# Attention and feed-forward block: value tiles 0 and 1 projected inside attention, output products of three groups ahead of the fourth division

## The chip, the cores and the metric

The kernel runs on one core of a Trainium2 chip, in one launch. The metric is the device time of that launch in microseconds (us). The median of three runs of the kernel before is the time to beat; a profiled execution gives the trace.

## What is computed

The block works on four sequences (B = 4) of 512 steps with 512 channels. In each of two stages a conditioning scan over time runs forward and backward in every channel and gives a ratio that is multiplied by a sigmoid of the input. The first stage is followed by causal attention with 16 heads of 32 channels, the second by a gated feed-forward layer with 2048 inner channels whose operands are quantised in blocks of 32. Cut to its core, the reference is:

```python
x = x + attn(cond(x, fside, fside, w, u, cond_512), w_qkv, w_o)
x = x + ffn(cond2(x, fside, fside, w2, u2, cond_512), w_gate, w_up, w_down)

# cond: nf, df are scans of ek*v and ek forward in time, nb, db backward
num = nf + nb - ekv + euk * vf
den = df + db - ek + euk
base = sigmoid(r) * (num / maximum(den, 1e-08))

# attn
q, k, v = split(einsum('bsh,oh->bso', hidden, w_qkv))
probs = softmax(where(causal, q @ k.T * scale, min))
out = einsum('bsh,oh->bso', probs @ v, w_o)

# ffn: every operand is rounded to a 4- or 6-bit grid with one power of two per block of 32
inter = silu(mx(x, w_gate)) * mx(x, w_up)
out = mx(inter, w_down)
```

## The kernel before

All arrays have the channels on the 128 partitions, in four chunks (`CJ = 4`), and time on the free axis. The program is written engine by engine with an order fixed by hand; semaphores join the engines. `turn(b, more)` exists on every engine and does sequence `b`, from the attention's second half of preparations to the output. `more` is false in the last turn (b = 3).

**Matmuls.** TensorE (PE) first does the scores by query of a head group (`scores`, six slots of a group, banks 0 to 3), whose maxima VectorE (DVE) takes (`maxima`). After `split_maxima` the maxima are transposed (`transpose_maxima`, bank 2), copied by ScalarE (ACT, `copy_maxima`), and used in the scores by key (`scores_by_key`, units n = 0 to 15 of a group, banks 4 and 5), which ACT turns into probabilities (`exps`). `weigh_values` multiplies the probabilities with the values `v_sb` and with ones into banks 6 and 7, and the division follows: a logarithm and an exponential on ACT (`sum_reciprocal`), three operations on DVE (`normalise`). Four groups (g = 0 to 3) run like this, and the six slots of the next group's `scores` stand between the units of the present one (`SLOT_BEHIND`). Groups 2 and 3 of the queries and keys are projected into banks 6 and 7 and copied out of there by `copy_raw`, which counts on `raw_copied`.

**The tail of a turn.** Behind the fourth group PE projects value tiles 0 and 1 of the next sequence, waits for the fourth division (`normed`), does the output projection (16 fp32 products of 128x512, each of which the trace shows as two instructions), value tiles 2 and 3, and queries and keys of group 0 of the next sequence. DVE adds each output chunk to `xt`, ACT takes its tanh (`tanh2`), DVE joins it to the second stage's ratio (`join`), makes the block scales and rounds. That sets `xq_ready`, for which the gate products (L1179) wait.

**The scans.** Between all of this DVE and ACT run the conditioning scans, unit by unit (`forward`, `backward`, `add_own`, `finish` on DVE, `weigh`, `reciprocals`, `own_exp` on ACT). Units 4 to 7 of a turn make `h` of the next sequence, units 8 to 11 the second stage's ratios of that sequence. In the last turn none of them is done. `h` is one buffer: SyncE (SP) loads `x[b + 1]` into it as soon as the queries and keys of turn b have been projected, and ACT takes its tanh behind group 0's exponentials.

GpSimd (POOL) makes two low parts at the head of a turn and issues half of the DMAs that place queries and keys in `stacks`.

## Time and profile before

| | |
|---|---|
| median of three runs | 1052.24 us (1050.89 to 1053.39) |
| profiled execution, time | 1056.65 us |
| profiled execution, span of the core | 1054.8 us |
| mean granted TensorE clock | 0.913 of full |
| PE busy | 729.8 us (69%) |
| DVE busy | 852.9 us (81%) |
| ACT busy | 414.6 us (39%) |
| shares of the chain that ended last | PE 42%, DVE 39%, issue 11%, ACT 7% |

The span runs from the first to the last instruction of the core. Busy times of engines overlap. The chain is followed back from the last instruction, at each step to what released it. A row of the timeline gives the start in us from the span's start, the length, the engine, the line of the kernel, the operation with output and inputs, how many instructions are merged (x), and in brackets the idle time of the engine ahead of it with what ended that. The granted clock is a share of 2.4 GHz; 0.50 is 1.2 GHz. The first 245 us of the span prepare the weights; the turns begin at about 245, 449, 656 and 861 us.

### The profile page before, as it was taken

The page shows a single profiled execution, that of the slowest core. Times are in us where ns is not written, and L with a number is a line of the kernel's source. Part 1 is how long each engine was busy: PE and PEld are TensorE (multiplying, and loading weights), DVE is VectorE, ACT ScalarE, POOL GpSimd, SP SyncE. Part 2 cuts the span into 40 slices and gives each one's busy share as a digit, 9 for nine tenths or more (in the row PEclk, how much of TensorE's full clock was granted, in tenths as well). Part 3 has the DMA queues.
Part 4 walks back from the last instruction along what each step waited for, and adds up shares of the span by engine and source line. Part 5 has one row for each costly group of instructions (what it writes and reads, how often), then busy time and mean ns, then how long its engine had stood idle before and what let it go on. Part 6 is the DMA issues. An engine that isn't in the chain of part 4 may idle for free.

```text
span 1054.8 us, 10177 instructions
## 1 busy us (share of the span) xinstructions
PE 729.8 (69%) x3680; PEld 366.4 (35%) x3680; DVE 852.9 (81%) x1160; ACT 414.6 (39%) x698; POOL 94.2 (9%) x151
## 2 busy tenths in 40 slices
PE   0000003835787899978789999778899996987566
PEld 0000001313454444445444444445344444553222
DVE  5999999997899678898984788979858988532577
ACT  3010110313676435247663361465643515452140
POOL 1000000001310000131100001311000032200000
PEclk9999999877699999988968999878899997999688
DMA  8411211034340000364300004732000065400001
GB/s 328 174 66 40 90 50 40 24 76 128 87 105 11 21 0 11 80 210 97 93 21 11 1 10 101 212 97 71 21 10 1 11 161 126 113 1 0 1 1 40
DMA packets 30306, 72.24 MB, mean 68 GB/s; under 512 B 5808, under 2 KB 5808, under 8 KB 28464
## 3 DMA queue, kind: packets, MB, share of 16 engines
q1 hardware_dynamic: 19792, 46.94, 14.9%
q0 software_dynamic: 6144, 16.79, 6.7%
q10 hardware_dynamic: 4320, 7.87, 2.3%
q8 instruction: 29, 0.48, 0.2%
q14 instruction: 21, 0.17, 0.1%
HBM read 33.82 MB, written 4.19 MB: 36 GB/s over the span
## 4 chain that ended last, share of the span: by engine, by line
PE 42%; DVE 39%; issue 11%; ACT 7%; DMA 1%; SPq 0%; ACTq 0%; DVEq 0%
PE bank L1179 11%; PE bank L1158 5%; PE bank L1119 5%; PE bank L1046 4%; PE bank L1103 4%; PE bank L1053 3%; PE bank L1079 3%; DVE region L691 3%; DVE negmax L866 2%; ACT region L475 2%; PE bank L1104 2%; DVE ratio L670 2%; DVE region L671 2%; DVE num L769 2%; DVE ratio L645 2%
## 5 line engine op out<-in xcount | busy, mean ns | idle before, releaser
L1046 PE MATMUL bank<-wqkv,h 128*128 128x512 f32 x128 | 60.0, 623 | 179.5 <-DVE h L803 171.0
L1103 PE MATMUL bank<-stacks 128*128 128x512 f32 (+3 forms) x256 | 115.8, 454 | 50.6 <-ACT region L475 42.0
L273 POOL DMA_DIRECT2D stacks<-rows x128 | 70.1, 555 | 778.4 <-DVE region L671 384.1
L866 DVE TENSOR_REDUCE negmax<-bank 128x4 f32<-128x512 f32 (+2 forms) x96 | 99.3, 1035 | 43.2 <-PE bank L1081 42.9
L475 ACT ACTIVATE region<-bank 128x512 f32<-128x512 f32 (+3 forms) x256 | 101.6, 433 | 81.1 <-PE bank L1105 80.3
L1053 PE MATMUL bank<-h,wqkv 128*128 128x512 f32 x256 | 113.7, 595 | 4.2 <-DVE region L1011 4.2
L1046 PEld LDWEIGHTS bank<-wqkv,h 128*128 128x128 f32 x128 | 25.2, 201 | 211.1 <-issue 201.7
L1079 PE MATMUL bank<-stacks 128*128 128x128 f32 (+3 forms) x256 | 94.6, 449 | 5.6 <-DVE negmax L866 4.4
L1104 PE MATMUL bank<-maxrow,pick 128*128 128x512 bf16 (+3 forms) x256 | 90.5, 353 | 0.0
L1103 PEld LDWEIGHTS bank<-stacks 128*128 128x128 f32 x256 | 56.5, 221 | 84.3 <-ACT region L475 62.1
L410 ACT ACTIVATE rec<-den 128x512 f32<-128x512 f32 x32 | 20.1, 630 | 145.6 <-DVE den L780 144.5
L1179 PE MATMUL bank<-region,gate_q 128*128 128x512 bf16 x256 | 62.2, 387 | 14.2 <-DVE region L671 14.2
L1191 PE MATMUL bank<-region,down_q 128*128 128x512 bf16 x256 | 59.0, 387 | 16.2 <-DVE region L671 16.2
L1053 PEld LDWEIGHTS bank<-h,wqkv 128*128 128x128 f32 x256 | 47.9, 190 | 60.6 <-issue 54.5
L1011 DVE TENSOR_TENSOR region<-bank,region 128x1024 f32<-128x1024 f32 x32 | 39.0, 1219 | 31.7 <-PE bank L1179 31.7
L1079 PEld LDWEIGHTS bank<-stacks 128*128 128x128 f32 x256 | 58.0, 229 | 14.4 <-issue 6.8
L1081 PE MATMUL bank<-hide_qk,identb 128*128 128x128 bf16 x256 | 62.4, 249 | 0.0
L1105 PE MATMUL bank<-hide_kq,identb 128*128 128x128 bf16 x256 | 62.0, 242 | 0.0
L1179 PE MATMUL bank<-region,up_q 128*128 128x512 bf16 x256 | 61.5, 384 | 0.0
L1158 PE MATMUL bank<-rows,wo 128*128 128x512 f32 x128 | 57.4, 607 | 3.5 <-DVE rows L884 3.5
L394 ACT ACTIVATE fd<-fd,omd_all 128x511 f32<-128x511 f32 x32 | 22.9, 716 | 93.5 <-DVE fd L752 93.5
L1119 PE MATMUL bank<-region,v_sb 128*32 128x128 f32 (+3 forms) x512 | 54.3, 485 | 1.8 <-ACT region L475 1.8
(126 smaller groups left out, 1378.8 us busy)
## 6 DMA issues: line engine op xcount, KB each, us to landing
stacks<-rows SPq DMA_DIRECT2D x128, 128.0 KB, 4.0
stacks<-rows POOLq DMA_DIRECT2D x128, 128.0 KB, 3.8
kt<-in_fside ACTq DMA_DIRECT2D x30, 256.0 KB, 3.1
h<-in_x SPq DMA_DIRECT2D x4, 1024.0 KB, 7.6
region<-in_w_gate SPq DMA_DIRECT2D x4, 1024.0 KB, 12.0
xt<-in_x SPq DMA_DIRECT2D x4, 1024.0 KB, 7.0
region<-in_w_up SPq DMA_DIRECT2D x4, 1024.0 KB, 5.6
region<-in_w_down SPq DMA_DIRECT2D x4, 1024.0 KB, 4.7
```

The lines of the kernel that those rows point to most:

```text
L273: eng.dma_start(stacks[HD * r:HD * r + HD, at:at + 2, i, :].bitcast(F32), rows[mine, q:k + 1:k - q, :]).then_inc(stacked[s][i], 16)
L475: nc.scalar.activation(probs[:, i, P_AT[t]:P_AT[t] + CAUSAL[t]], bank[4 + n % 2][:, 0:CAUSAL[t]], ACT.Exp, scale=SCALE).then_inc(p_ready, 1)
L866: nc.vector.tensor_reduce(o, scored, AX_X, ALU.max, negate=True).then_inc(max_taken, 1)
L1046: mm = nc.tensor.matmul(bank[4 + t % 2][:, :], h[:, j, P * t:P * t + P], wqkv[:, j, 2 * C:3 * C], start=(j == 0), stop=(j == CJ - 1))
L1053: mm = nc.tensor.matmul(qk_banks(g)[s][:, :], wqkv[:, j, C * s + P * g:C * s + P * g + P], h[:, j, :], start=(j == 0), stop=(j == CJ - 1))
L1079: nc.tensor.matmul(o[:, c:c + w], qs[s][:, i, P * t:P * t + P], ks[s][:, i, 0:w], start=True, stop=False, skip_group_check=True)
L1081: mm = nc.tensor.matmul(o[:, c + P * t:c + w], identb[:, :], hide_qk[:, :], start=False, stop=True, skip_group_check=True)
L1103: nc.tensor.matmul(o, ks[s][:, i, P * t:P * t + P], qs[s][:, i, P * t:T], start=True, stop=False)
L1104: nc.tensor.matmul(o, pick[:, i, :], maxrow[:, s, P * t:T], start=False, stop=False)
L1119: mm = nc.tensor.matmul(o[HD * i:HD * i + HD, P * t:T], w, probs[:, i, P_AT[t]:P_AT[t] + CAUSAL[t]], start=(t == 0), stop=(t == TT - 1), t ...
L1158: mm = nc.tensor.matmul(bank[j][:, :], wo[:, g, P * j:P * j + P], attn[g], start=(g == 0), stop=(g == GROUPS - 1))
L1179: mm = nc.tensor.matmul(bank[4 * (f % 2) + o + i][:, :], w[:, j, at:at + P], xq[:, j, :], start=(j == 0), stop=(j == CJ - 1))
```

## The change

- `project_values` now does one tile. Tiles 2 and 3 are projected where they were (and in the prologue), tiles 0 and 1 inside the attention part of the turn that uses them: tile 0 behind the last slot of group 0's `scores` and ahead of `transpose_maxima(b, 0)`, tile 1 behind unit 9 of group 0's `scores_by_key`. They go to banks 6 and 7 (`value_bank`) and wait for `raw_copied`.
- ACT copies tile 0 behind `copy_maxima(b, 0)` and tile 1 behind group 0's last exponentials. `weigh_values` of group 0 waits for both copies (`v_copied`) where it waited for `raw_copied`.
- The output projection is done by `project_out`: the products of groups 0 to 2 of chunks 0 and 1 come ahead of the first product that waits for the fourth division, and each chunk's fourth product comes behind the next chunk's first three.
- On DVE, unit 8's `backward` and `add_own` stand ahead of `normalise(b, 3)`.
- SP loads `h` of the next sequence when all four value tiles of the present one are done (`v_ready`), and it issues group 2's stack DMAs ahead of that wait.

```diff
+        def value_bank(t):
+
+            return bank[4 + t % 2] if t >= 2 else bank[6 + t]
...
+                stack(sp, b, 2, 0, 2)
                 if more:
-                    sp.wait_ge(qk_ready, b * (2 * GROUPS) + 2 * GROUPS)
+                    sp.wait_ge(v_ready, b * TT + TT)
                     sp.dma_start(h[:, :, :], x[b + 1]).then_inc(h_in, 16)
-                for g in range(2, GROUPS):
-                    stack(sp, b, g, 0, 2)
+                stack(sp, b, 3, 0, 2)
...
                 copy_maxima(b, 0)
+                copy_values(b, (0,))
                 weigh(b, 3, 1)
...
                 exps(b, 0, 10, 16)
+                copy_values(b, (1,))
                 weigh(b, 4, 0)
...
                 own_exp(b, 9)
-                if more:
-                    copy_values(b + 1, 0, 2)
...
                 cap(b, 9)
-                normalise(b, 3)
                 backward(b, 8, 0)
                 backward(b, 8, 1)
                 add_own(b, 8)
+                normalise(b, 3)
...
+            def project_values(b, t):
+
+                if t >= 2:
+                    pe.wait_ge(h_ready, b * CJ + CJ)
+                else:
+                    pe.wait_ge(raw_copied, 2 * b + 2)
...
-                        pe.wait_ge(raw_copied, 2 * b + 2)
+                        pe.wait_ge(v_copied, b * TT + TT)
...
+            def project_out(b, j, groups):
+
+                for g in groups:
+                    if g == GROUPS - 1:
+                        pe.wait_ge(normed, b * GROUPS + GROUPS)
+                    mm = nc.tensor.matmul(bank[j][:, :], wo[:, g, P * j:P * j + P], attn[g],
+                                          start=(g == 0), stop=(g == GROUPS - 1), skip_group_check=True)
+                if g == GROUPS - 1:
+                    mm.then_inc(proj_ready, 1)
...
                 scores(b, 0, 5)
+                project_values(b, 0)
                 transpose_maxima(b, 0)
...
+                        if g == 0 and n == 9:
+                            project_values(b, 1)
...
+                for j in range(CJ):
+                    project_out(b, j, range(GROUPS - 1))
+                    if j:
+                        project_out(b, j - 1, (GROUPS - 1,))
+                project_out(b, CJ - 1, (GROUPS - 1,))
                 if more:
-                    project_values(b + 1, 0, 2)
-                pe.wait_ge(normed, b * GROUPS + GROUPS)
-                for j in range(CJ):
-                    for g in range(GROUPS):
-                        mm = nc.tensor.matmul(bank[j][:, :], wo[:, g, P * j:P * j + P], attn[g],
-                                              start=(g == 0), stop=(g == GROUPS - 1))
-                    mm.then_inc(proj_ready, 1)
-                if more:
-                    project_values(b + 1, 2, TT)
+                    for t in (2, 3):
+                        project_values(b + 1, t)
```

On PE, at the tail of turn 0, behind the last products with the values, before the change (`wqkv,h` are value products, `rows,wo` output products):

```order
L1119 MATMUL bank<-region,ones 32x128 x4
L1046 MATMUL bank<-wqkv,h 128x512 [waits h_ready]
L1046 MATMUL bank<-wqkv,h 128x512 x7
L1158 MATMUL bank<-rows,wo 128x512 [waits normed]
L1158 MATMUL bank<-rows,wo 128x512 x15
L1046 MATMUL bank<-wqkv,h 128x512 [waits v_copied,h_ready]
L1046 MATMUL bank<-wqkv,h 128x512 x3
```

The same place on PE after the change:

```order
L1124 MATMUL bank<-region,ones 32x128 x4
L1135 MATMUL bank<-rows,wo 128x512 x6
L1135 MATMUL bank<-rows,wo 128x512 [waits normed]
L1135 MATMUL bank<-rows,wo 128x512 x3
L1135 MATMUL bank<-rows,wo 128x512 [waits normed]
L1135 MATMUL bank<-rows,wo 128x512 x3
L1135 MATMUL bank<-rows,wo 128x512 [waits normed] x2
L1051 MATMUL bank<-wqkv,h 128x512 [waits h_ready]
```

Eight value products are gone from here, and six output products now stand ahead of the first wait for the division.

On PE, at the head of turn 0, between group 0's last scores and its first unit by key, before the change:

```order
L1079 MATMUL bank<-stacks_49 128x512
L1081 MATMUL bank<-hide_qk,identb 128x128
L1088 MATMUL bank<-identb,negmax_hl 8x128 [waits max_split]
L1088 MATMUL bank<-identb,negmax_hl 8x128 x3
L1103 MATMUL bank<-stacks_49 128x512 [waits qk_low,mt_copied]
```

The same place on PE after the change:

```order
L1084 MATMUL bank<-stacks_49 128x512
L1086 MATMUL bank<-hide_qk,identb 128x128
L1051 MATMUL bank<-wqkv,h 128x512 [waits raw_copied]
L1051 MATMUL bank<-wqkv,h 128x512 x3
L1093 MATMUL bank<-identb,negmax_hl 8x128 [waits max_split]
L1093 MATMUL bank<-identb,negmax_hl 8x128 x3
L1108 MATMUL bank<-stacks_49 128x512 [waits qk_low,mt_copied]
```

Value tile 0 stands between the scores and the transposes, and it waits for ACT's raw copy.

On DVE, at the tail of turn 0, after the change (`rows<-bank,rsum` and its two neighbours are the division, `den`, `num` and `ekv` unit 8):

```order
L743 TENSOR_SCALAR ek<-kt 128x512 [waits fwd_ready,k_in1]
L773 SCALAR_TENSOR_TENSOR den<-decay_all,fd 128x512 [waits weighted,fwd_ready,h_ready,divided]
L773 SCALAR_TENSOR_TENSOR num<-decay_all,fn 128x512 [waits fwd_ready,weighted]
L782 SCALAR_TENSOR_TENSOR ekv<-eu,kt 128x512 [waits eu_ready]
L784 SCALAR_TENSOR_TENSOR den<-eu,den 128x512 [waits bwd_ready]
L787 TENSOR_TENSOR num<-num,ekv 128x512 [waits bwd_ready,euv_ready]
L884 TENSOR_TENSOR rows<-bank,rsum 128x512 [waits rsum_ready]
L886 SCALAR_TENSOR_TENSOR rsum<-rows,rsum 128x512 [waits refined]
L888 SCALAR_TENSOR_TENSOR rows<-bank,rsum 128x512 [waits refined]
L997 TENSOR_TENSOR xt<-bank,xt 128x512 [waits proj_ready,x_in]
```

The three rows of the division stood ahead of the five rows of unit 8 and now stand behind them.

## Rows read from the trace of the kernel before

**Rows 1.** Windows of attention, turn 1 and turn 3: length, busy time of each engine.

```profile
480.00:548.00 68.00, 55.54 (x428) 31.70 (x426) 64.06 (x86) 45.79 (x89) 8.46 (x16) 0.89 0.28 70
...
900.00:950.00 50.00, 45.98 (x412) 27.45 (x404) 22.31 (x31) 23.65 (x57) 5.62 (x11) 1.00 0.23 54
```

**Rows 2.** The chain that ended last, turn 1's tail: start, length, what.

```profile
554.94 7.05 PE bank L1119 x64
...
561.99 7.06 PE bank L1046 x16
...
569.05 13.73 PE bank L1158 x32
...
582.79 6.87 PE bank L1046 x16
...
596.52 1.81 PE bank L1059 x4
```

**Rows 3.** Timeline of PE, turn 3's tail: start, length, what, idle before it.

```profile
958.26 15.70 PE L1158 MATMUL bank<-rows,wo 128*128 128x512 f32 x32 [3.55 <-DVE rows L884]
...
988.17 3.59 PE L1179 MATMUL bank<-region,gate_q 128*128 128x512 bf16 x8 [14.21 <-DVE region L671]
```

**Rows 4.** Timeline of DVE, turn 1's tail.

```profile
563.34 0.69 DVE L880 TENSOR_TENSOR rows<-bank,rsum 128x512 f32<-128x512 f32 x1 [8.14 <-ACT rsum L492]
...
568.84 0.68 DVE L783 TENSOR_TENSOR num<-num,ekv 128x512 f32<-128x512 f32 x1
...
576.57 1.22 DVE L755 TENSOR_TENSOR_SCAN fn<-decay_all,ekv 128x512 f32<-128x512 f32 x1
...
581.03 0.69 DVE L985 SCALAR_TENSOR_TENSOR ratio<-region,ratio 128x512 f32<-128x512 f32 x1 [0.95 <-ACT region L575]
...
582.89 0.69 DVE L993 TENSOR_TENSOR xt<-bank,xt 128x512 f32<-128x512 f32 x1 [0.71 <-PE bank L1158]
...
595.73 1.23 DVE L671 TENSOR_TENSOR region<-ratio,region 128x2048 bf16<-128x2048 bf16 x1
```

**Rows 5.** Timeline of ACT, turn 1's tail.

```profile
571.89 1.06 ACT L437 ACTIVATE v_sb<-bank 128x512 f32<-128x512 f32 x2
```

**Rows 6.** Timeline of ACT, PE and DVE at turn 1's head.

```profile
465.50 1.00 ACT L463 ACTIVATE rows<-bank 128x1024 f32<-128x1024 f32 x1
...
469.14 0.80 PE L1103 MATMUL bank<-stacks 128*128 128x512 f32 x1 [2.13 <-ACT maxrow L469]
...
466.19 0.17 DVE L873 TENSOR_TENSOR negmax_hl<-negmax,negmax_hl 128x16 bf16<-128x16 f32 x1
...
480.47 0.68 DVE L780 SCALAR_TENSOR_TENSOR den<-eu,den 128x512 f32<-128x512 f32 x1
```

**Rows 7.** Timeline of DVE, turn 2's head.

```profile
673.10 0.17 DVE L873 TENSOR_TENSOR negmax_hl<-negmax,negmax_hl 128x16 bf16<-128x16 f32 x1
...
686.20 0.68 DVE L780 SCALAR_TENSOR_TENSOR den<-eu,den 128x512 f32<-128x512 f32 x1
```

**Rows 8.** Windows of one us: busy times, PEclk is the granted clock.

```profile
478.00:479.00 1.00, 1.00 (x10) 0.75 (x9) 0.09 (x1) 0.99 (x3) 0.00 (x0) 0.91 0.06 16
...
679.00:680.00 1.00, 1.00 (x9) 0.95 (x9) 1.00 (x1) 0.00 (x0) 0.97 (x1) 0.72 0.00 0
...
962.00:963.00 1.00, 1.00 (x2) 0.34 (x1) 0.00 (x0) 0.00 (x0) 0.00 (x0) 0.56 0.00 0
```

**Rows 9.** Timeline of PE: thirteenth unit of group 0, turns 1 to 3.

```profile
484.55 0.50 PE L1103 MATMUL bank<-stacks 128*128 128x512 f32 x1 [3.05 <-ACT region L475]
...
690.27 0.80 PE L1103 MATMUL bank<-stacks 128*128 128x512 f32 x1 [4.08 <-ACT region L475]
...
896.00 0.50 PE L1103 MATMUL bank<-stacks 128*128 128x512 f32 x1 [2.10 <-ACT region L475]
```

**Rows 10.** Instructions on h, 450 to 562 us: its load's time to landing.

```profile
DMA to landing us min/median/max: 8.3/8.3/8.3
```

**Rows 11.** Timeline of ACT: the tanh of h in turn 1.

```profile
491.65 1.92 ACT L518 ACTIVATE h<-h 128x2048 f32<-128x2048 f32 x1
```

More of the change, by code:

```diff
@@ L433, in _, with copy_values @@
             table(6)
-            def copy_values(b, first, last):
-                for t in range(first, last):
-                    act.wait_ge(v_ready, b * TT + t + 1)
-                    nc.scalar.activation(v_sb[:, t, :], bank[4 + t % 2][:, :], ACT.Copy).then_inc(v_copied, 1)
+            def copy_values(b, tiles):
+                for t in tiles:
+                    act.wait_ge(v_ready, b * TT + VALUE_ORDER.index(t) + 1)
+                    nc.scalar.activation(v_sb[:, t, :], value_bank(t)[:, :], ACT.Copy).then_inc(v_copied, 1)
             def high_parts(b, g):
@@ L576, in turn @@
                 if more:
-                    copy_values(b + 1, 2, TT)
+                    copy_values(b + 1, (2, 3))
                     high_parts(b + 1, 0)
@@ L618, in _ @@
                 if u == 8:
-                    copy_values(0, 0, TT)
+                    copy_values(0, (2, 3))
                     high_parts(0, 0)
@@ L1039, in _ @@
         def _(pe):
-            def project_values(b, first, last):
-                pe.wait_ge(h_ready, b * CJ + CJ)
-                for t in range(first, last):
-                    if t >= 2:
-                        pe.wait_ge(v_copied, b * TT + t - 1)
-                    for j in range(CJ):
-                        mm = nc.tensor.matmul(bank[4 + t % 2][:, :], h[:, j, P * t:P * t + P], wqkv[:, j, 2 * C:3 * C],
-                                              start=(j == 0), stop=(j == CJ - 1))
-                    mm.then_inc(v_ready, 1)
+            def project_values(b, t):
[4 more added lines that the diff above has]
+                for j in range(CJ):
+                    mm = nc.tensor.matmul(value_bank(t)[:, :], h[:, j, P * t:P * t + P], wqkv[:, j, 2 * C:3 * C],
+                                          start=(j == 0), stop=(j == CJ - 1))
+                mm.then_inc(v_ready, 1)
             def project_qk(b, g, s):
@@ L1151, in turn @@
                         scores(b, g + 2, 1)
-                if more:
-                    project_values(b + 1, 0, 2)
-                pe.wait_ge(normed, b * GROUPS + GROUPS)
-                for j in range(CJ):
-                    for g in range(GROUPS):
-                        mm = nc.tensor.matmul(bank[j][:, :], wo[:, g, P * j:P * j + P], attn[g],
-                                              start=(g == 0), stop=(g == GROUPS - 1))
-                    mm.then_inc(proj_ready, 1)
-                if more:
-                    project_values(b + 1, 2, TT)
+                for j in range(CJ):
+                    project_out(b, j, range(GROUPS - 1))
+                    if j:
+                        project_out(b, j - 1, (GROUPS - 1,))
+                project_out(b, CJ - 1, (GROUPS - 1,))
+                if more:
+                    for t in (2, 3):
+                        project_values(b + 1, t)
                     for s in range(2):
@@ L1198, in _ @@
             pe.wait_ge(weights_in, 32)
-            project_values(0, 0, TT)
+            for t in (2, 3):
+                project_values(0, t)
             for s in range(2):
@@ L1203, in _ @@
                 leave_low(0, 0, s)
-            pe.wait_ge(v_copied, TT)
+            pe.wait_ge(v_copied, 2)
             for s in range(2):
@@ L1216 @@
 HIGHS, LOWS = 6, 6
+VALUE_ORDER = (2, 3, 0, 1)
 SLOT_BEHIND = ({1: 0, 3: 1, 6: 2, 9: 3, 12: 4, 15: 5}, {3: 2, 7: 3, 11: 4, 15: 5})
```

2 lines of the change are left out of this document (1 added, 1 removed).

## The prediction

> **What bounds the kernel now.** I read first the chain that ended last, then the windows by stage, then the timelines at the two places where the order changes. The turns differ inside. Through most of attention in turns 0 to 2 DVE is the bound: busy 64.06 of 68 us in turn 1, PE 55.54. In turn 3, without scans of a next sequence, DVE has 22.31 us of work in 50, and PE with 45.98 is the bound [rows 1]. At a tail the chain lies on PE alone: values times probabilities until 561.99, two value tiles (7.06), the output projection (13.73), two more value tiles (6.87), then queries, keys and low parts until 598.33, where the gate products begin [rows 2]. Turns 0 and 2 have the same pieces to 0.1 us. In turn 3 nothing fills the wait: PE idles 3.55 us for the division, the projection takes 15.70 us in place of 13.73, and PE then idles 14.21 us for `xq_ready` [rows 3].
>
> **The tail, turns 0 to 2.** I count from T, the end of the last weighing of values (561.99). Removed from PE is 7.06 us. One product costs 13.73/16 = 0.86. Six products now fill 5.15 us. The division needs 3.5 us from T (the idle time of [rows 3]), so it comes in time. It also needs DVE to be free. Unit 8's two scans and three additions, which now stand ahead of it, take from 565.4 to 569.5, 4.1 us, and DVE has a hole of 8.14 us ahead of the division [rows 4], so they cost nothing. Were the hole gone, the division would be up to 4.1 us late, of which 5.15 - 3.5 = 1.65 is covered.
>
> The projection ends at T + 13.7. The chunks are ready after 7, 11, 15 and 16 products: T + 6.0, 9.4, 12.9 and 13.7. PE's remaining fill is 598.33 - 582.79 = 15.54 us [rows 2], so PE could begin the gates at T + 29.3. The other chain runs over DVE and ACT. Unit 9's second forward scan comes 0.6 us behind the addition of chunk 1, so at T + 10.2, and ends at T + 11.4. Behind it ACT weighs the scan, does `cap_exp`, loads a table and takes the first tanh. From the scan's end (576.57 + 1.22) to the first join (581.03) that took 3.2 us [rows 4]. The first join follows at T + 14.6 and takes until 15.8 (from 581.03 to 582.2), and only then comes the addition of chunk 3. From that addition to the end of the rounding it took 596.96 - 582.89 = 14.07 [rows 4]. So `xq_ready` comes at T + 29.9, 0.6 us behind PE. Before it was T + 36.3. Each of three tails gains 6.4 us: 19.2.
>
> **The tail, turn 3.** T is 954.7. The gates began at 988.17, T + 33.5 [rows 3]. There is no unit 9 and the table is loaded early, so the join of chunk 0 begins right after the addition of chunk 2, at T + 13.7, chunk 3 is added at T + 14.8 and the gates begin at T + 28.9. Gain 4.6, of which 3.5 is the filled wait and 2.0 the low clock behind it, less 0.9 because chunks 2 and 3 now come 0.86 us apart. Sum of the tails: 19.2 + 4.6 = 23.8.
>
> **The head: value tile 0.** It doesn't fill the idle time in which it stands. PE is done with the scores about 4 us ahead of the transposes, but the tile waits for the raw copy, which ACT ends at 466.50, and the maxima are split at 466.36 [rows 6]. So the tile begins when the transposes began before and puts all of its own length ahead of them. That length is 3.43 us at full clock (6.87/2) and 6.87 at half. After this idle time the granted clock is at half in all four turns. In turn 3's tail the clock came back in the window 962 to 963 [rows 8], about 4.6 us after the products had begun at 958.26. I take that: 4.6 us at 0.86 per instruction are 5.4 of the tile's 8, the other 2.6 take 1.1, in all 5.7 us. Transposes and the copy of the maxima add about 1.0. PE so begins the units by key at 473.2 in place of 469.14, 4.1 us later. In exchange it is at full clock. Before, it ran at half until the window 478 to 479 [rows 6, 8], 9.0 us whose work takes 4.5 at full clock. 473.2 + 4.5 = 477.7 is level with 478.2. I book 0.
>
> What follows is DVE's: the next thing that ACT's reciprocals wait for is unit 3's denominator, 480.47 + 0.68, which is 14.8 us behind the split in turn 1 and 13.6 in turn 2, where DVE had no hole [rows 6, 7]. Walking the slots through, I get 15.0 for every turn: +0.2 in turn 1, +1.4 in turn 2, and about as before in turns 0 and 3.
>
> The Trainium skill (TensorE: Matmul & The Clock Gate, Terms) prices low clock at its length times one half. In turn 2 PE began its units 2.8 us behind the split, at 676.05, and was back at full clock in the window 679 to 680 [rows 8], so it had 3.5 us at half against turn 1's 9.0. By the rule turn 1 should lose 2.8 us more than turn 2; the rows show 1.2, since DVE has its own 13.6 us there. By the rule a tile that brought the clock back would be worth 4.5 us in a turn, by the rows 1.2.
>
> **The head: value tile 1.** PE waited 3.05, 4.08 and 2.10 us ahead of unit 12 in turns 1, 2 and 3 [rows 9], while ACT did unit 3's reciprocals; turn 0 is like turn 1. The tile takes 3.4 us at full clock. It fits in turn 2. In turns 0 and 1 it is 0.4 too long, and units 10 and 11 (0.6 us) and an exponential now come behind it: +1 us for unit 12. But PE no longer idles, and where it did it fell to half clock: the same product took 0.80 us in turn 2 and 0.50 in turn 1. That returns 0.3 us on this product alone and more on those behind it, about what these delays cost. I book 0 for turns 0 to 2. In turn 3 the hole was 2.1 us, no low clock stood behind it, and PE is the bound: +1.5 us, and 0.3 for the copy of the tile.
>
> **The small ones.** ACT's copies take 0.6 each (1.06 for two, [rows 5]). The one behind the last exponentials holds the first weighing of values and the tanh of `h` by 0.6 us; DVE hides it in turns 0 to 2. The load of `h` begins at about 484.6 in place of 461.2. It took 8.3 us while it shared the queues with `xt` [rows 10], so it lands by 492.9 at worst; the tanh began at 491.65 [rows 11] and would now at 492.2. I take no wait, since it now flies almost alone; the bound is 1 us on ACT in each of three turns. Behind the waiting tanh stand a table load and the copy of group 1's maxima, for which PE waits. The prologue loses two tiles that lay under the weights' quantisation: 0.
>
> **Sum.** -19.2 - 4.6 + 0 + 1.8 = -22.0 us. The profiled execution took 1056.65, which gives 1034.7. The runs' median is 1052.24, 4.4 lower, and what I changed are orders of work that all runs share: 1030.2. A difference under 0.2% (2.1 us) would be no difference here.
>
> **Rivals.** (a) *The head is dearer* (0.22). Tile 0 runs wholly at half clock (+1.2), the tanh waits for `h` (+1), or the slots behind cost DVE what I called hidden: 2 to 4 us in each turn, in all 8 to 16 more less what the clock returns. For it speaks that both tiles stand in a part where DVE had no slack to give; against it, that DVE waited for PE at these very places. It gives 1038 to 1046, at 3 us a turn 1042. (b) *The head gives back* (0.14). The clock returns early enough that DVE's own 13.6 us bind in turns 0 and 1 too, and no low clock follows tile 1: -1.2 in each of three turns, and turn 3's +1.8 is paid the same way. 1052.2 - 23.8 - 3.6 = 1024.8. By the skill's price of 4.5 us a turn it would be 1015, which the rows of turn 2 speak against. (c) *Slower than before* (0.03). The clock stays at half through group 0, as it did for 9 us of dense work in turn 1. Then PE begins 5.5 us late, gains nothing, and tile 1 takes 6.9 in a hole of 3: +3.9. That is over 8 us a turn, 33 in all against 23.8: about 1061. It decides from 6 us a turn. (d) *The fill is hidden anyway* (0.05): `xq_ready` comes no earlier since its chain is held by ACT and DVE work of unit 9, and the tails return 2 us each: 1052 - 12 + 2 = 1042. Against it speaks that the chain has nothing on it that isn't counted above.
>
> **The numbers.** My forecast (0.56) has its own range of 1026 to 1035. To reach 8 in 10 I take in (b) and most of (a): 1023 to 1042. Faster by over 0.2%: all but (c), and a little for what I haven't seen, 0.95; within 0.2% 0.02; slower 0.03.
>
> **What the trace after would show.** Right: the output products begin within 0.1 us of the last weighing in all four turns and run without a hole; the gates begin 29 to 30 us behind that in turns 0 to 2, 29 in turn 3; tile 0 begins at the end of the raw copy, with the first instructions at 0.86 us; the tanh of `h` follows the table load at once. Wrong: the tails not 6.4 shorter; split to unit 3's denominator over 17 us; a wait of ACT for `h`; attention from the split to T longer by more than 2 us in a turn.

## The result, and the profile after

The changed kernel takes 1033.76 us in the median of four runs (1032.72 to 1035.09); the kernel before took 1052.76 in four (1050.89 to 1053.39). The ratio is 0.9823 with an interval of 0.9806 to 0.9841, so 19.0 us less. The prediction was 1030.2 with a range of 1023 to 1042. The two sets of runs don't overlap, and 19.0 us is 1.8% of the time. The profiled execution took 1032.72 us, its span 1030.9; the mean granted clock rose from 0.913 to 0.942, and PE's busy time fell from 729.8 to 706.6 us for the same 3680 matmuls.

The changed kernel's page, engines and costliest groups, shows that no product of the output projection waits any more:

```profile
PE 706.6 (69%) x3680; PEld 350.1 (34%) x3680; DVE 852.4 (83%) x1160; ACT 411.5 (40%) x698; POOL 94.1 (9%) x151
...
L1195 PE MATMUL bank<-region,gate_q 128*128 128x512 bf16 x256 | 62.2, 387 | 16.8 <-DVE region L675 16.8
...
L1135 PE MATMUL bank<-rows,wo 128*128 128x512 f32 x128 | 56.0, 595 | 0.0
```

**The tails.** PE in turn 1, where [rows 2] has 36.2 us from the end of the weighing to the gates (line L1179 before, L1195 now). Columns: start, length, what, and in brackets the idle time ahead.

```profile
554.22 14.00 PE L1135 MATMUL bank<-rows,wo 128*128 128x512 f32 x32
568.06 7.03 PE L1051 MATMUL bank<-wqkv,h 128*128 128x512 f32 x16
574.92 7.03 PE L1058 MATMUL bank<-h,wqkv 128*128 128x512 f32 x16
581.79 1.98 PE L1064 MATMUL bank<-rows,less_ident 128*128 128x512 f32 x4
584.34 1.90 PE L1195 MATMUL bank<-region,gate_q 128*128 128x512 bf16 x8 [0.57 <-DVE region L675]
```

The same in turn 3, against [rows 3]:

```profile
936.19 14.00 PE L1135 MATMUL bank<-rows,wo 128*128 128x512 f32 x32
965.26 3.56 PE L1195 MATMUL bank<-region,gate_q 128*128 128x512 bf16 x8 [15.07 <-DVE region L675]
```

DVE in turn 1's tail, against [rows 4]:

```profile
555.64 0.69 DVE L884 TENSOR_TENSOR rows<-bank,rsum 128x512 f32<-128x512 f32 x1 [3.40 <-ACT rsum L496]
...
563.97 0.69 DVE L997 TENSOR_TENSOR xt<-bank,xt 128x512 f32<-128x512 f32 x1 [0.94 <-PE bank L1135]
564.57 1.22 DVE L759 TENSOR_TENSOR_SCAN fn<-decay_all,ekv 128x512 f32<-128x512 f32 x1
...
569.04 0.69 DVE L989 SCALAR_TENSOR_TENSOR ratio<-region,ratio 128x512 f32<-128x512 f32 x1 [0.95 <-ACT region L579]
...
570.22 0.69 DVE L997 TENSOR_TENSOR xt<-bank,xt 128x512 f32<-128x512 f32 x1
...
583.05 1.22 DVE L675 TENSOR_TENSOR region<-ratio,region 128x2048 bf16<-128x2048 bf16 x1
```

PE passes from the weighing into 16 output products without a hole. The division still waits 3.40 us for ACT, with unit 8 now ahead of it. Counted from T (554.35, the start of ACT's logarithm of the fourth sums, level with the end of the weighing), the scan begins at T + 10.2, the first join at T + 14.7, the addition of chunk 3 at T + 15.9 and the gates at T + 30.0. PE was ready 0.57 us earlier. The prediction had 10.2, 14.6, 15.8, 29.9 and 0.6.

**The head.** Turn 1, PE and DVE, against [rows 6]:

```profile
461.83 6.20 PE L1051 MATMUL bank<-wqkv,h 128*128 128x512 f32 x8 [4.00 <-ACT rows L467]
...
469.02 0.50 PE L1108 MATMUL bank<-stacks 128*128 128x512 f32 x1 [0.68 <-ACT maxrow L473]
...
476.55 0.68 DVE L784 SCALAR_TENSOR_TENSOR den<-eu,den 128x512 f32<-128x512 f32 x1
476.77 3.65 PE L1051 MATMUL bank<-wqkv,h 128*128 128x512 f32 x8
...
481.19 0.50 PE L1108 MATMUL bank<-stacks 128*128 128x512 f32 x1 [0.23 <-ACT region L479]
...
490.45 0.30 PE L1084 MATMUL bank<-stacks 128*128 128x128 f32 x1 [0.69 <-DMA stacks<-rows]
```

Tile 0 waits for the raw copy and takes 6.2 us, mostly at half clock. The maxima were split at 461.65, so PE begins the units by key 7.4 us behind the split, and unit 3's denominator ends 15.6 behind it (476.55 + 0.68); in turns 0, 2 and 3 it is 15.7, 15.7 and 15.5. Tile 1 takes the place of the idle time of [rows 9]: unit 12 now waits 0.23 us, at full clock. The last row is one that nothing foretold: the scores of group 2 wait for a stack DMA. Experiments 7, 8 and 9 bear on it.

The windows of one us show the clock. Before, it stayed at half until the window 478 to 479 [rows 8]; now it is back 5 us behind the tile's start:

```profile
462.00:463.00 1.00, 1.00 (x2) 0.48 (x3) 1.00 (x2) 1.00 (x2) 0.00 (x0) 0.50 0.32 131
...
466.00:467.00 1.00, 1.00 (x2) 0.34 (x1) 0.96 (x2) 0.00 (x0) 1.00 (x1) 0.56 0.00 0
467.00:468.00 1.00, 1.00 (x4) 0.23 (x3) 1.00 (x1) 0.00 (x0) 1.00 (x1) 1.00 0.00 0
```

**Where the time came from.** This table is made from the starts and ends of single rows, in us. Its first stretch runs from the split of group 0's maxima to that of group 1's, its last from T to the first gate product. "Again" is the same kernel profiled once more (below). From the gates to the next split both kernels take 75.1, and 75.1 to 75.4 into turn 3.

| stretch | kernel, run | turn 0 | turn 1 | turn 2 | turn 3 |
|---|---|---|---|---|---|
| split 0 to split 1 | before | 25.29 | 24.83 | 24.88 | 23.10 |
| | after | 25.08 | 24.98 | 25.05 | 24.88 |
| split 0 to T | before | 91.14 | 95.69 | 93.82 | 76.47 |
| | before, again | 91.76 | 92.39 | 93.82 | 76.47 |
| | after | 93.11 | 92.70 | 92.89 | 78.61 |
| T to the gates | before, both | 36.12 | 36.12 | 36.12 | 33.40 |
| | after | 29.98 | 29.99 | 29.99 | 28.94 |

The tails return 3 x 6.13 + 4.46 = 22.9 us. Attention (split 0 to T) adds up to 357.1 in the first profile of before, 354.4 in the second and 357.3 after. The profile of the changed kernel in experiment 11 has 93.45, 93.93, 92.99 and 77.97 us there, in all 358.4, with the tails at 29.99, 30.00, 29.99 and 28.94. So the tails repeat, and attention cost 2.9 or 3.9 us against the second profile of before, 0.2 or 1.2 against the first.

Two stretches outside the table got shorter too. The first split comes at 263.4 in place of 264.0 (264.4 again), and behind turn 3's first gates the span runs for 65.7 us in place of 66.7.

### The profile page after: what moved, and what is told of

It is laid out like the page before. It is cut to its first block, busy times and chain, and to the rows that moved or that the text cites. A ratio compares the mean times of both kernels' runs of the same rounds, so it can differ in the third digit from the quotient of the medians.

```text
span 1030.9 us, 10174 instructions
## 1 busy us (share of the span) xinstructions
PE 706.6 (69%) x3680; PEld 350.1 (34%) x3680; DVE 852.4 (83%) x1160; ACT 411.5 (40%) x698; POOL 94.1 (9%) x151
## 4 chain that ended last, share of the span: by engine, by line
DVE 43%; PE 35%; issue 12%; ACT 7%; DMA 2%; POOL 0%; SPq 0%; DVEq 0%; ACTq 0%
PE bank L1195 11%; PE bank L1124 4%; PE bank L1135 4%; PE bank L1051 4%; PE bank L1108 3%; DVE region L695 3%; ACT region L479 3%; DVE negmax L870 2%; PE bank L1084 2%; DVE ratio L674 2%; DVE region L675 2%; DVE num L773 2%; DVE ratio L649 2%; DVE region L656 2%; DVE region L657 2%
## 5 line engine op out<-in xcount | busy, mean ns | idle before, releaser
L1051 PE MATMUL bank<-wqkv,h 128*128 128x512 f32 x128 | 70.7, 709 | 186.9 <-DVE h L807 170.9
L1108 PE MATMUL bank<-stacks 128*128 128x512 f32 (+3 forms) x256 | 105.6, 414 | 37.7 <-ACT region L479 35.0
L479 ACT ACTIVATE region<-bank 128x512 f32<-128x512 f32 (+3 forms) x256 | 98.9, 433 | 60.7 <-PE bank L1110 60.5
L1051 PEld LDWEIGHTS bank<-wqkv,h 128*128 128x128 f32 x128 | 28.5, 230 | 221.9 <-issue 205.3
L1084 PE MATMUL bank<-stacks 128*128 128x128 f32 (+3 forms) x256 | 83.4, 407 | 7.7 <-DVE negmax L870 4.4
L1109 PE MATMUL bank<-maxrow,pick 128*128 128x512 bf16 (+3 forms) x256 | 80.9, 316 | 0.0
L1195 PE MATMUL bank<-region,gate_q 128*128 128x512 bf16 x256 | 62.2, 387 | 16.8 <-DVE region L675 16.8
L1108 PEld LDWEIGHTS bank<-stacks 128*128 128x128 f32 x256 | 49.8, 194 | 68.2 <-ACT region L479 53.5
L1207 PE MATMUL bank<-region,down_q 128*128 128x512 bf16 x256 | 60.0, 393 | 15.5 <-DVE region L675 15.5
L398 ACT ACTIVATE fd<-fd,omd_all 128x511 f32<-128x511 f32 x32 | 22.9, 717 | 106.3 <-DVE fd L756 106.3
L1195 PE MATMUL bank<-region,up_q 128*128 128x512 bf16 x256 | 60.5, 379 | 0.0
L1110 PE MATMUL bank<-hide_kq,identb 128*128 128x128 bf16 x256 | 57.0, 223 | 0.0
L1086 PE MATMUL bank<-hide_qk,identb 128*128 128x128 bf16 x256 | 56.9, 230 | 0.0
L1084 PEld LDWEIGHTS bank<-stacks 128*128 128x128 f32 x256 | 50.1, 199 | 15.9 <-issue 8.4
L589 ACT ACTIVATE region<-bank 128x1024 f32<-128x1024 f32 x32 | 32.7, 1021 | 56.9 <-PE bank L1195 56.9
```

The costliest lines, as they stand in the source:

```text
L479: nc.scalar.activation(probs[:, i, P_AT[t]:P_AT[t] + CAUSAL[t]], bank[4 + n % 2][:, 0:CAUSAL[t]], ACT.Exp, scale=SCALE).then_inc(p_ready, 1)
L1051: mm = nc.tensor.matmul(value_bank(t)[:, :], h[:, j, P * t:P * t + P], wqkv[:, j, 2 * C:3 * C], start=(j == 0), stop=(j == CJ - 1))
L1084: nc.tensor.matmul(o[:, c:c + w], qs[s][:, i, P * t:P * t + P], ks[s][:, i, 0:w], start=True, stop=False, skip_group_check=True)
L1108: nc.tensor.matmul(o, ks[s][:, i, P * t:P * t + P], qs[s][:, i, P * t:T], start=True, stop=False)
L1109: nc.tensor.matmul(o, pick[:, i, :], maxrow[:, s, P * t:T], start=False, stop=False)
L1110: nc.tensor.matmul(o[:, 0:P], identb[:, :], hide_kq[:, :], start=False, stop=True).then_inc(st_ready, 1)
```

## The experiments

All ratios are to the kernel before in runs on the same chip, with a 95% interval. Three chips were used; the kernel before took 1052.1, 1052.0 and 1050.8 us on them.

**1. The kernel before, unchanged.**

> The kernel before, unchanged, profiled a second time. My theory: the first profiled execution (span 1054.8 us) was slower than the usual run because turn 1's fourth group ran at half clock; in another execution the time from the last split of the maxima to the end of the last weighing of values is 21 to 23 us in turns 0 to 2 (it was 21.1, 26.1 and 22.6), and the span is 1049 to 1052. Rival: the excess is the profiler's own, and the same places come out again, span 1054 to 1055.

Measured: 1051.4 us (10 runs), 0.9995 (0.9975 to 1.0015), span 1052.5, 0.5 us above the expected range. The window from the fourth split to T in turn 1, in the first profile of before and in this one:

```profile
536.00:562.00 26.00, 22.48 (x169) 11.27 (x161) 16.09 (x22) 13.07 (x27) 0.00 (x0) 0.67 0.04 12
```

```profile
537.00:560.00 23.00, 17.80 (x149) 9.32 (x150) 16.06 (x23) 12.88 (x28) 0.00 (x0) 0.85 0.04 13
```

Columns behind the length: busy PE, weight loads, DVE, ACT, POOL, then the granted clock. DVE and ACT do the same work. PE is busy 4.7 us longer at a clock of 0.67 than at 0.85, and not all of that is the clock's: it was late already and had 20 more instructions in this window, 16 of them products of group 2 with the values, which take 1.5 us and in the second profile stood ahead of the split. The stretch took 26.1 us and 22.7. One profile of this kernel thus fixes nothing under 3 us in one turn; the tails, and the first stretch of a head in turns 1 to 3, repeat to 0.1 us, while turn 0's first stretch was 25.29 and 23.95.

**2. The fill undone.** The value tiles stay inside attention, but the output products stand in the old order, all 16 behind the wait for the division.

```diff
                 for j in range(CJ):
-                    project_out(b, j, range(GROUPS - 1))
-                    if j:
-                        project_out(b, j - 1, (GROUPS - 1,))
-                project_out(b, CJ - 1, (GROUPS - 1,))
+                    project_out(b, j, range(GROUPS))
```

> The changed kernel with the output products in their old order, all behind the wait for the fourth division; value tiles stay in attention. My theory (the fill is worth the wait and the low clock behind it): gates begin 34.5 to 35 us behind the end of the weighing in turns 0 to 2 (30.0 with the fill) and 33.4 in turn 3 (28.9), total 16 to 20 us above the changed kernel, about 1052. Rival (moving the value tiles is what gains, the fill matters little since ACT and DVE lead the chain): under 8 us above it.

Measured: 1052.11 us (10 runs), 0.9986 (0.9968 to 1.0004), so all of the gain is gone. PE in turn 1's tail:

```profile
563.16 15.70 PE L1135 MATMUL bank<-rows,wo 128*128 128x512 f32 x32 [3.55 <-DVE rows L888]
578.70 7.03 PE L1051 MATMUL bank<-wqkv,h 128*128 128x512 f32 x16
...
594.25 1.89 PE L1193 MATMUL bank<-region,gate_q 128*128 128x512 bf16 x8
```

The two tiles left the tail, and in their place came what [rows 3] show for turn 3: 3.55 us idle, and 15.70 us for products that need 13.73. The gates came at T + 34.57, against 36.12 with the tiles. So 7.06 us of removed work returned 1.55 in each of three tails. Of these 4.7 us the profiled span shows 3.4 (1049.1 against run 1's 1052.5) and the medians nothing, so attention (355.7 us in this profile, 354.4 in run 1's) and the spread of the runs took the rest. The fill is worth 3 x 4.58 + 4.45 = 18.2 us by these marks, 18.4 by the median of the changed kernel's first runs and 19.2 by that of experiment 4, on the same chip.

**3. The fill alone.** The kernel before with the new order of output products and unit 8 ahead of the division; all four value tiles stand behind the projection.

```diff
                 if more:
-                    project_values(b + 1, 0, 2)
-                pe.wait_ge(normed, b * GROUPS + GROUPS)
+                    project_values(b + 1, 0, TT)
```

> The kernel before with the new order of the output products and of unit 8 on DVE, but all four value tiles behind the projection. My theory (PE's own length bounds turns 0 to 2, so the fill gains there only because two tiles left the tail): turns 0 to 2 as before, gates 36 us behind the end of the weighing, turn 3 gains 4.5: 1048. Rival (the chain over DVE and ACT is what was shortened): turns 0 to 2 gain too, 1042 or less.

Measured: 1046.16 us (10 runs), 0.9955 (0.9937 to 0.9973). The gates come at T + 36.12 in turns 0 to 2, as before, and at T + 28.94 in turn 3. PE in turn 1's tail:

```profile
558.13 14.00 PE L1128 MATMUL bank<-rows,wo 128*128 128x512 f32 x32
571.97 13.90 PE L1044 MATMUL bank<-wqkv,h 128*128 128x512 f32 x32
585.70 7.03 PE L1051 MATMUL bank<-h,wqkv 128*128 128x512 f32 x16
592.57 1.98 PE L1057 MATMUL bank<-rows,less_ident 128*128 128x512 f32 x4
594.38 1.89 PE L1184 MATMUL bank<-region,gate_q 128*128 128x512 bf16 x8
```

And the last operation of DVE's chain, which sets `xq_ready`:

```profile
586.96 1.23 DVE L669 TENSOR_TENSOR region<-ratio,region 128x2048 bf16<-128x2048 bf16 x1
```

T is 558.26 here, so the fill alone brought `xq_ready` from T + 34.9 ([rows 4]) to T + 29.9, where the whole change has it too. The gates gained nothing by it, because PE was full until T + 36.1. The gates wait for the later of two chains. The fill alone shortens that of `xq_ready` and not PE's own; the value tiles alone shorten PE's, but the wait for the division takes most of it back (experiment 2). Half of the change alone returns 6 us or nothing; both together return 19. Of the 6 us, turn 3's tail accounts for 4.5; the expected total was 1048, and where the other 2 us lie was not followed up.

**4. The division ahead of unit 8, as before.**

```diff
                 cap(b, 9)
+                normalise(b, 3)
                 backward(b, 8, 0)
                 backward(b, 8, 1)
                 add_own(b, 8)
-                normalise(b, 3)
```

> The changed kernel with the fourth division ahead of unit 8's scans on DVE again. My theory: the division is on time either way, unit 8 ends 4.1 us behind it, the first addition comes 1.5 us later, most of it is lost again by the third: 0 to 0.7 us per turn in three turns, total +0 to +2. Rival (DVE leads the tail): the gates come 1.5 us or more later in each of turns 0 to 2, total +4 or more.

Measured: 1032.88 us (4 runs), 0.981 (0.9786 to 0.9835); the gates at T + 30.06, 30.06, 30.07 and 28.94. Moving unit 8 is worth 0.07 us in each of three turns, below what can be measured.

**5. Value tile 0 from one of its four products.** Left out: three quarters of the sum of tile 0, so its values are incomplete.

```diff
+                first = CJ - 1 if t == 0 else 0
-                for j in range(CJ):
+                for j in range(first, CJ):
```

> The changed kernel with value tile 0 made from one of its four products, so three quarters of its computation are left out: this measures what the tile costs at the head. It still begins when the raw copy ends, at half clock. My theory: the tile takes 1.7 us in place of 6.2, so PE begins the units 4.5 us earlier but at half clock, and unit 3's denominator comes 1.2 to 1.4 us nearer to the split in some turns and not at all in others (DVE's own 13.6 us bind): total -1 to -5. Rival (the head pays the tile in full): -4.5 in each of four turns, -16 or more.

Measured: 1032.99 us (4 runs), 0.983 (0.9798 to 0.9861). That is 0.8 us under the changed kernel's first median, on another chip, where 1 to 5 were expected: no gain that can be told. The profiled execution was the slowest of the four (1037.13), with a fourth group of 26.1 us in turn 1 as in run 1; the heads are read from it. Timeline and windows of turn 1's head:

```profile
462.83 2.07 PE L1052 MATMUL bank<-wqkv,h 128*128 128x512 f32 x2 [4.00 <-ACT rows L467]
...
466.10 0.79 PE L1109 MATMUL bank<-stacks 128*128 128x512 f32 x1 [0.68 <-ACT maxrow L473]
```

```profile
474.00:475.00 1.00, 1.00 (x6) 0.61 (x6) 1.00 (x1) 0.72 (x2) 0.00 (x0) 0.55 0.67 156
475.00:476.00 1.00, 1.00 (x10) 0.69 (x8) 0.20 (x2) 0.95 (x3) 0.00 (x0) 1.00 0.00 0
```

PE was through the tile about 4 us earlier, but its clock then stayed at half until 475, 12 us behind the tile's start in place of 5. The run doesn't isolate the tile's length: it took the length away and the clock's early return with it. It is the same in all four turns: full clock returned 12.0 to 12.9 us behind the split, against 5.1 to 5.5 in the change, and the first stretch took 25.04, 24.90, 24.90 and 24.59 us against 25.08, 24.98, 25.05 and 24.88. That work and clock balance is what the prediction booked (0) for the whole tile.

**6. Tile 0 in bank 5, ahead of the wait for the raw copy.** Nothing is left out. The tile goes to a bank that is free behind group 0's scores, waits for the low parts (`qk_low`) alone, and unit 1, which uses bank 5, waits for its copy.

```diff
-            return bank[4 + t % 2] if t >= 2 else bank[6 + t]
+            return (bank[5], bank[7], bank[4], bank[5])[t]
...
+                elif t == 0:
+                    pe.wait_ge(qk_low, b * LOWS + 4)
...
+                if g == 0 and n == 1:
+                    pe.wait_ge(v_copied, b * TT + 3)
```

> The changed kernel with value tile 0 in bank 5, waiting for the low parts of group 1 in place of the raw copy; unit 1 of group 0 waits for its copy. Nothing is left out. My theory: the tile runs inside the idle time ahead of the transposes (3.4 us at full clock), the clock doesn't fall, the transposes start when the maxima are split, and unit 3's denominator comes 13.6 to 14 us behind the split in place of 15.0: -1 to -1.4 us in each of turns 0 to 2, -1.5 to -3 in turn 3 which PE bounds, total -5 to -7, about 1027. Rival (it isn't where the tile stands but how much PE has to do in attention): within 2 us of the changed kernel.

Measured: 1027.49 us (4 runs), 0.9768 (0.9741 to 0.9794). Repeated on a third chip (run 10) with

> tile0_bank5 again, beside both_ahead on the same chip: 1027 to 1028 as before, so that the two can be told apart.

it took 1021.59 us in the median of 6 (1021.48 to 1029.85), 0.9739 (0.9712 to 0.9767). PE at turn 1's head, and windows, from the repetition:

```profile
454.19 3.65 PE L1053 MATMUL bank<-wqkv,h 128*128 128x512 f32 x8
458.22 0.39 PE L1095 MATMUL bank<-identb,negmax_hl 128*8 128x128 bf16 x4 [0.38 <-DVE negmax_hl L877]
460.94 0.49 PE L1112 MATMUL bank<-stacks 128*128 128x512 f32 x1 [2.33 <-ACT maxrow L473]
```

```profile
464.00:465.00 1.00, 1.00 (x8) 0.81 (x5) 1.00 (x1) 0.48 (x2) 0.86 (x1) 0.50 0.00 0
...
469.00:470.00 1.00, 1.00 (x8) 0.80 (x7) 0.96 (x2) 0.35 (x2) 0.00 (x0) 0.79 0.00 0
```

The expectation of 1027 to 1028 was missed by 6 us, and the same program has medians of 1027.5 and 1021.6 on two chips, a difference that stays unexplained. Here the tile does fill the idle time in which it stands: eight instructions in 3.65 us at full clock, and the units by key begin 2.8 us behind the split (458.16) in place of 7.4. From the first split to the second the four turns took 23.5, 23.15, 23.15 and 23.1 us, against 25.0 of the change, and attention as a whole 346.4 in place of 357.3. Of these 10.9 us, 7.1 lie in the four first stretches; 4.3 lie behind the fourth split in turns 0 to 2 (21.1 us each in place of 22.5), where nothing was moved. "The clock doesn't fall" was wrong: half clock still follows, from about 463 to 469. In the first of the two runs the first stretches were 22.4, 24.3, 24.4 and 21.1 (7.7 less than in the change) and attention 351.2.

**7. Value tile 1 from one of four products.** Left out: three quarters of the sum of tile 1.

```diff
+                first = CJ - 1 if t == 1 else 0
```

> The changed kernel with value tile 1 made from one of its four products, so three quarters of its computation are left out. My theory: 2.6 us less of PE work in a hole of 3 us; turns 0 to 2 change by less than 1 us each, since the clock may fall again; turn 3, where the hole is 2.1 us, gains 1.5: total -1 to -3. Rival (tile 1 is paid in full): -2.6 in each of four turns, -10.

Measured: 1033.87 us (4 runs), 0.9837 (0.9807 to 0.9866). The expected 1 to 3 us didn't show. Split 0 to split 1 was shorter in turns 0, 1 and 3 (23.4, 23.6, 25.2, 22.6), but turn 1's T came at 95.8, 3 us later than in the change. The reason is in that turn's trace, and it isn't tile 1's length. The scores of group 2 waited for a stack DMA as in the changed kernel, but for 4.78 us, and the chain that ended last runs over that DMA:

```profile
493.11 0.44 PE L1085 MATMUL bank<-stacks 128*128 128x128 f32 x1 [4.78 <-DMA stacks<-rows]
...
484.63 8.24 DMA stacks<-rows
```

The load of `h` beside it, issued at 477.85, took 13.0 us to land (5.2 in turn 1 of the changed kernel), and ACT's tanh of `h` waited 4.8 us for it too. The shorter tile had put the load 2.5 us closer to the split. The run is inconclusive on what tile 1 costs, and shows what the load can cost.

**8. Only a quarter of `h` is loaded.** Left out: three of four chunks of the next sequence's `x`, which thus keep old contents.

```diff
-                    sp.dma_start(h[:, :, :], x[b + 1]).then_inc(h_in, 16)
+                    sp.dma_start(h[:, 0:1, :], x[b + 1, :, 0:1, :]).then_inc(h_in, 16)
```

> The changed kernel with only a quarter of h loaded from memory for the next sequence, so the values behind it are others: this takes the late load out of the way of group 2's stack DMAs. My theory, formed from the trace after: PE's wait of 0.7 to 0.8 us for stacks ahead of group 2's first scores, new in turns 0 to 2, is the last stack DMAs sharing the queues with the load of h (landing 4.3 us against 3.4 or less before), and it goes away: total -1 to -2. Rival (the stack DMAs are issued too late by POOL whatever else flies): the wait stays, total within 0.5 us.

Measured: 1029.95 us (4 runs), 0.9796 (0.9761 to 0.983); split 0 to T took 91.11, 91.62, 90.90 and 78.26, in all 5.4 us less than in the changed kernel. 5.1 of the 5.4 lie in turns 0 to 2; turn 3, which loads no `h`, hardly moves. (The tails only look 0.2 to 0.4 us longer in the profiles of this chip: these have records of 61 of a turn's 64 products with `gate_q` and lack the first, while `xq_ready`'s last operation ends at T + 29.9 and 28.9 as in the changed kernel.) In the changed kernel the chain that ended last runs over the stack DMA, here in turn 2:

```profile
682.37 1.58 POOL stacks L277 x3
683.95 4.27 DMA stacks<-rows
...
688.46 0.30 PE bank L1084
```

SP issues `h` and POOL the stacks of group 2 within a few us:

```profile
480.45 0.34 SPq L313 DMA_DIRECT2D h<-in_x  x1
```

```profile
481.56 2.14 POOL L277 DMA_DIRECT2D stacks<-rows  x4 [13.24 <-PE bank L1110]
484.49 2.12 POOL L277 DMA_DIRECT2D stacks<-rows  x4 [0.78 <-PE bank L1110]
```

In the changed kernel PE waits 1.18, 0.69 and 0.82 us for them in turns 0 to 2; with a quarter of `h` the scores of group 2 begin without a DMA wait in all three, here in turn 1:

```profile
487.17 0.33 PE L1084 MATMUL bank<-stacks 128*128 128x128 f32 x1
```

The medians differ by 3.8 us from the changed kernel's, on different chips and with intervals that overlap. That the late load costs PE its wait is shown by the rows. What it costs in the end is better read from the stretch that has the wait in it, from the second split to the third, in turns 0, 1 and 2:

| kernel | turn 0 | turn 1 | turn 2 |
|---|---|---|---|
| before, both profiles | 22.74 | 22.74 | 24.25 |
| a quarter of `h` (experiment 8) | 22.74 | 22.73 | 22.74 |
| `h` ahead of the stacks (experiment 9) | 22.74 | 22.74 | 22.74 |
| changed | 23.56 | 23.09 | 23.20 |
| changed, again (experiment 11) | 23.71 | 23.96 | 23.82 |
| tile 1 from a quarter (experiment 7) | 23.74 | 28.03 | 22.80 |

By this the late load costs 1.6 us over three turns in the first profile of the change and 3.3 in the second. (The 24.25 of before began with 1.9 us at half clock; with it the stretch as a whole hardly grew in the first profile.) Of the other 3.8 us of the 5.4, 2.9 lie behind the fourth split, in the stretch that run 1 showed to vary, and aren't the load's by any row.

**9. Tile 0 in bank 5, tile 1 behind the transposes, `h` loaded ahead of group 2's stacks.**

```diff
                 transpose_maxima(b, 0)
+                project_values(b, 1)
...
-                        if g == 0 and n == 9:
-                            project_values(b, 1)
...
-                stack(sp, b, 2, 0, 2)
                 if more:
                     sp.wait_ge(v_ready, b * TT + TT)
                     sp.dma_start(h[:, :, :], x[b + 1]).then_inc(h_in, 16)
+                stack(sp, b, 2, 0, 2)
```

> The kernel with value tile 0 in bank 5 (as in tile0_bank5), value tile 1 right behind the transposes of group 0, and the load of h ahead of group 2's stack DMAs. My theory: tile 1 begins in PE's 2.1 us wait for the copied maxima and puts the units 1 to 1.5 us later, hidden by DVE; h is loaded some 10 us earlier, away from group 2's stacks, which gave 1.2 us a turn in h_quarter; against it, the hole ahead of unit 12 is empty again and the clock may fall behind it: 1024 to 1027, a little below tile0_bank5. Rival (the filled hole ahead of unit 12 was worth more than the collision): 1029 or more.

Measured: 1025.89 us (4 runs), 0.976 (0.9742 to 0.9778). PE in turn 1's head:

```profile
459.55 3.70 PE L1053 MATMUL bank<-wqkv,h 128*128 128x512 f32 x8
...
476.19 0.80 PE L1112 MATMUL bank<-stacks 128*128 128x512 f32 x1 [4.70 <-ACT region L479]
```

The load of `h` is out of the way, and no scores of group 2 wait for a stack DMA in any turn, with nothing left out. But tile 1 no longer stands where PE waits for ACT: a hole of 4.70 us is back ahead of unit 12, with half clock behind it (0.80 us for a product of 0.50), as in [rows 9]. Against the expectation, this kernel isn't below experiment 6's: on the same chip that one was 4.3 us faster in the medians, with intervals that overlap. Which of the two is faster isn't settled; both beat the change.

**10.** is the repetition of 6, told there.

**11. The changed kernel once more, on the third chip.**

> The changed kernel again, on the chip on which both_ahead and bank5_again run: 1032 to 1034 us, as it was on its first chip.

Measured: 1033.67 us (4 runs), 0.9832 (0.9813 to 0.9851). It and the two better versions shared the runs of before, so experiment 6's gain over the change, 12.1 us in these medians, is not one of the chip; on the second chip it was 6.3 against the change's first median. The intervals of the ratios on the third chip don't overlap (0.9712 to 0.9767 and 0.9813 to 0.9851).

## Why the prediction was right, and 3.5 us too low

- **What bounds the kernel.** Right. DVE is busy 64.2 of the 68 us from 480 to 548 in the changed kernel too (64.06 before, [rows 1]).
- **The tails, the term that carries the sum.** The mechanism is shown by experiments 2 and 3, and its stations by the rows of after to 0.1 us. The size was off by a little: 6.13 a turn where 6.4 was taken, 22.9 in all for 23.8. The step that failed is the "before" end of the difference: the gates were taken to begin at 598.33, where their first row starts at 598.17, and T, by the start of ACT's logarithm, lies 0.06 later than the prediction's; that makes T + 36.12. And T + 29.9 was 29.98.
- **Unit 8 ahead of the division costs nothing.** Right (experiment 4).
- **Tile 0.** Predicted start at the raw copy's end: right. Its length was put at 5.7 us and was 6.2, PE's restart at 4.1 us later than before and was 4.6, and so unit 3's denominator at 15.0 us behind the split and was 15.6. Booked at 0 for turns 0 to 2, and the first stretch of the head moved by -0.2, +0.15 and +0.17. Experiment 5 agrees with the reason given, that the late start and the early return of the clock cancel. The exactness is luck: against the second profile of before turn 0 moved by +1.1, and in the changed kernel's second profile turn 2 took 24.17 in place of 25.05. The Trainium skill (TensorE: Matmul & The Clock Gate, Terms) takes half clock at half its length. By that rule the 9.0 us of before would be worth 4.5. The rows here can't test it, since the tile's work, its own half clock and DVE's work are mixed in them; they show 0.2 us in all.
- **Tile 1.** Predicted 0 in turns 0 to 2 and +1.8 in turn 3; turn 3's first stretch grew by 1.78, from 23.10 to 24.88. The number is right by luck. In the changed kernel's second profile the stretch took 24.14, 1.0 more than before, and in the repetition of experiment 6, where tile 1 stands where it does in the change and only tile 0 is elsewhere, it took 23.12: the growth was gone with tile 0, for which the prediction had booked nothing. Turn 3's attention as a whole grew by 2.1 us, just over the 2 that the prediction named as a sign of being wrong.
- **The load of `h`.** "I take no wait" was right for ACT, whose tanh follows the table load in 487.52 at once. It was the wrong question. The load was followed to its own reader only, and not to the stack DMAs that now fly beside it: PE waits 0.7 to 1.2 us for these in turns 0 to 2, and the table of experiment 8 puts the whole at 1.6 to 3.3 us. This is the term left out of the sum. That the load "flies almost alone" was wrong, and experiment 7 shows how far it can go: 13.0 us to landing and a wait of ACT too.
- **From the profile to the median.** The difference of the profiled executions, 1056.65 - 1032.72 = 23.9, is larger than that of the medians, 19.0. The step "what I changed are orders of work that all runs share" holds for the change and not for the one execution it was subtracted from. Attention took 357.1 us there and 354.4 in the second profile, with the half clock in other places (experiment 1). By the second profile: 22.9 of the tails less 2.9 in attention is 20.0. The spans differ by 21.6 there, since the prologue (1.0) and the stretch behind the last gates (1.0) got shorter as well, for neither of which the prediction had a term, and the stretches from the gates to the next split got longer by 0.3. The medians, with 19.0, have less than this; run 1's profiled execution, 1054.35, was itself 3 us above the median of its runs.

Together: of the 3.5 us, 0.5 is the median of before, which four runs put at 1052.76 and not 1052.24, and 3.0 is the change's own. Less 0.9 of the tails and 1.1 for attention (2.9 by the second profile, 1.8 booked), 22.0 becomes 20.0. The last 1.0 isn't explained; the profiled spans show 1.6 more than 20.0, not less, and both are inside what one profile and the next differ by. Of the rivals, (a) was right that the head is dearer, but its price was 2 to 4 us a turn and the late load cost 0.4 to 1.2; (b) wasn't seen in the change, though experiment 6 reaches more than it by another way; (c) wasn't either, since the clock was back ahead of the units by key in every turn (its own two terms, 5.5 and 3.9 us, also add up to more than the 33 us that it states for four turns); (d) was wrong, since the chain of `xq_ready` moved as counted.

## What to carry to other kernels

Taking work away in front of a wait gains only what the wait doesn't take back: here 7 us of products returned 1.5 until other independent work filled the place, and then 6.1. Where two chains end at the same wait, work out both: the fill alone brought one of them 5 us forward and returned nothing in turns 0 to 2. When a piece is moved into an idle stretch, look at what it waits for: behind the raw copy tile 0 began only as the stretch ended, and the same tile in a bank that was free filled it and made the kernel 6 to 12 us faster. And when a transfer is moved, ask not only whether its reader has it in time, but which small transfers on the critical path now share the queues with it.

## What the runs showed of the hardware

- Behind an idle time of PE of about 4 us the granted clock stayed at half for very different lengths: some 5 us from tile 0's start in the changed kernel, 12 where the tile was a quarter as long, 9.0 and 3.5 from the first unit by key in turns 1 and 2 of before [rows 8]. In experiment 6's first run, where PE's only long idle time at the head is 2.3 us, it fell to half for some 10 us in turns 1 and 2, while in turn 3 it was 1.00 in every window of one us from 853 to 885, and split 0 to split 1 took 21.1 us. In turns 2 and 3 of the changed kernel's second profile it was 3.4 us long in place of 6.8, and those first stretches were 0.7 to 0.9 us shorter. What decides between these was not found.
- One stretch of the same program differed by 3.4 us in one turn (22.7 and 26.1 us, 1.5 us of it work that came late), while ten runs have a median within 0.8 us of the other 25 on the same chip (1051.4 and 1052.1).
- The load of 1024 KB into `h` landed in 5.5 us in the median where it shares the queues with stack DMAs, and took 8.3 beside `xt` [rows 10]. A stack DMA beside it took 4.27 us on the chain that ended last. In experiment 7 such a load took 13.0 us and a stack DMA beside it 8.24.
